# A two-layer model on one core: how queries and keys are split into three bf16 parts in the second layer

## What is computed

```python
def _L1_attn_ref(x, spectral_basis, W_qkv, W_out, a, b, dt):
    ...
    def fhn_dynamics(stimulus, a, b, dt, n_steps=N_FHN_STEPS, tau=TAU, threshold=THRESHOLD):
        ...
        for _ in range(n_steps):
            dv_explicit = v - v * v * v / 3.0 - w + I
            v_next = v + dt * dv_explicit
            w_next = (w + alpha * (v_next + a)) / denom
            v = jnp.clip(v_next, -3.0, 3.0)
            w = jnp.clip(w_next, -3.0, 3.0)
        response = v * stim_scale
        ...
            scores = jnp.einsum('bhtd,bhsd->bhts', q_c, k_c) * scale
            probs = jax.nn.softmax(scores, axis=-1)
            attn_energy = probs.sum(axis=-1)
            stim = jnp.broadcast_to(attn_energy[..., None], (B, H, e - s, Dh))
            fhn_out, fhn_state = fhn_dynamics(stim, a, b, dt)
            fhn_gate = jax.nn.sigmoid(fhn_out.mean(axis=-1))[..., None]
            probs = probs * (0.5 + 0.5 * fhn_gate)
            probs = probs / (probs.sum(axis=-1, keepdims=True) + 1e-08)
            out_chunks.append(jnp.einsum('bhts,bhsd->bhtd', probs, v_c))
...
x = L0_attn_x                       # 16 x 512 x 128, float32
xn = _layernorm(x, axis=-1)
x = x + _L0_attn_ref(xn, ...) + _L0_ffn_ref(xn, ...)
xn = _layernorm(x, axis=-1)
x = x + _L1_attn_ref(xn, ...) + _L1_ffn_ref(xn, ...)
return x
```

## Time and profile before

| | |
|---|---|
| median of 3 runs | 1517.55 us (1516.59 to 1521.41) |
| profiled execution | 1515.43 us |
| its span, first to last instruction | 1513.5 us |
| TensorE, VectorE, ScalarE, GpSimd busy | 93%, 78%, 54%, 35% |
| mean granted TensorE clock | 0.984 |

### The profile page before, as it was taken

The page is one execution under the profiler, slowest core; times in us unless marked ns, Lnnn a source line. Parts: engine busy times, 40 slices in busy tenths (PEclk is TensorE's granted clock), DMA queues, the critical chain, the costliest instruction groups (busy, mean ns, idle before and its releaser), DMA issues.

```text
span 1513.5 us, 35393 instructions
## 1 busy us (share of the span) xinstructions
PE 1404.1 (93%) x12926; PEld 904.6 (60%) x12926; DVE 1177.3 (78%) x2687; ACT 817.2 (54%) x1562; POOL 523.3 (35%) x942
## 2 busy tenths in 40 slices
PE   5699999999999899999998999999999999999994
PEld 3467677677776799998884444444444444444432
DVE  4789889889888795456677888888888888888752
ACT  2334534544543333334334677777766777776673
POOL 2333234234233111172312244444434444442121
PEclk8999999999999999999999999999999999999997
DMA  4111111111112566776973444333334443332300
GB/s 119 38 42 52 45 48 44 51 47 44 54 33 66 165 208 209 220 245 208 258 195 62 98 106 105 98 98 102 87 93 102 108 103 97 98 92 70 82 9 14
DMA packets 118205, 151.94 MB, mean 100 GB/s; under 512 B 31269, under 2 KB 83109, under 8 KB 113413
## 3 DMA queue, kind: packets, MB, share of 16 engines
q1 hardware_dynamic: 105160, 119.47, 29.0%
q0 software_dynamic: 12880, 30.30, 6.8%
HBM read 108.35 MB, written 40.83 MB: 99 GB/s over the span
## 4 chain that ended last, share of the span: by engine, by line
PE 48%; DVE 32%; POOL 7%; issue 6%; ACT 5%; DMA 1%; SPq 0%; POOLq 0%; DVEq 0%; ACTq 0%
DVE nmax L1516 8%; PE bank L1948 8%; PE bank L1939 8%; DVE P L1205 7%; PE bank L1816 5%; PE bank L1994 5%; PE bank L2017 4%; ACT P L946 3%; PE bank L1773 3%; PE bank L1850 2%; PE bank L1957 2%; PE bank L1864 2%; DVE t L1080 1%; PE bank L2064 1%; DVE t L1078 1%
## 5 line engine op out<-in xcount | busy, mean ns | idle before, releaser
L1516 DVE TENSOR_REDUCE nmax<-bank 128x1 f32<-128x512 f32 (+3 forms) x704 | 428.8, 634 | 84.6 <-PE bank L1994 83.6
L946 ACT ACTIVATE P<-bank 128x512 f32<-128x512 f32 x640 | 371.2, 599 | 183.2 <-PE bank L2017 178.4
L1994 PE MATMUL bank<-KT,QT 76*128 76x512 bf16 (+3 forms) x1024 | 251.3, 303 | 28.5 <-DVE nmax L1516 20.9
L2017 PE MATMUL bank<-QT,KT 78*128 78x512 bf16 (+3 forms) x1024 | 244.5, 301 | 8.9 <-ACT P L946 5.5
L693 POOL DMA_INDIRECT xs_d<-xn,idx x128 | 124.6, 973 | 306.0 <-PE bank L1773 197.9
L1994 PEld LDWEIGHTS bank<-KT,QT 76*128 76x128 bf16 x1024 | 86.8, 97 | 189.1 <-DVE nmax L1516 130.6
L1816 PE MATMUL bank<-P,V 128*32 128x512 f32 (+3 forms) x2048 | 191.3, 447 | 0.0
L1205 DVE TENSOR_TENSOR P<-bank,early_w 128x512 f32<-128x512 f32 x256 | 158.7, 682 | 41.3 <-PE bank L1773 41.2
L910 ACT ACTIVATE hr<-bank 128x512 f32<-128x512 f32 x142 | 84.8, 597 | 175.0 <-PE bank L1939 172.1
L741 POOL DMA_INDIRECT hT<-ys_d,idx x104 | 103.5, 995 | 159.9 <-PE bank L2017 141.8
L2017 PEld LDWEIGHTS bank<-QT,KT 78*128 78x128 bf16 x1024 | 98.6, 98 | 85.0 <-ACT P L946 31.9
(11 more groups left out here) (257 smaller groups left out, 2228.6 us busy)
## 6 DMA issues: line engine op xcount, KB each, us to landing
QT<-parts_d SPq DMA_DIRECT2D x96, 192.0 KB
P<-in_fc SPq DMA_DIRECT2D x71, 256.0 KB, 2.9
P<-in_proj SPq DMA_DIRECT2D x71, 256.0 KB, 3.2
parts_d<-parts SPq DMA_DIRECT2D x32, 384.0 KB, 2.5
P<-xs_d SPq DMA_DIRECT2D x71, 128.0 KB, 3.0
ys_d<-P POOLq DMA_DIRECT2D x71, 128.0 KB, 3.4
KT<-parts_d SPq DMA_DIRECT2D x64, 128.0 KB
KT<-parts_d SPq DMA_DIRECT2D x32, 192.0 KB
```

Source lines behind the costliest of these rows:

```text
L946: nc.scalar.activation(P[s % 2][:, u, :], bank[k % 2][:, :], ACT.Exp, scale=float(DH) ** -0.5).then_inc(s_sb, 1)
L1516: nc.vector.tensor_reduce(nmax[:, s // TWO, h:h + TWO * nh - 1:TWO, j], max_bank(n, k)[:, 0:nh * w].rearrange("p (h w) -> p h w", h=nh), A ...
L1994: ins = pe.matmul(max_bank(n, k)[:, i * w:(i + 1) * w], QT[n.p][0:MROWS, h, j * 128:(j + 1) * 128], KT[n.p][0:MROWS, h, 0:w], start=True, ...
L2017: ins = pe.matmul(bank[k % 2][:, c:c + n], KT[b.p][0:SROWS, h, 128 * kb:128 * kb + 128], QT[b.p][0:SROWS, h, 128 * kb:T], start=True, stop ...
```

## The change

In the loop, `take_part` and `lo2` are gone. ScalarE copies the bank to `t1` in float32 (`raw2`, at (1,7) and (1,9)). GpSimd subtracts the high part from `t1` in place (`residue_of`, both c, after the gather at unit 16 and ahead of `fhn_two_steps`). `mid2` casts `t1` in place of the bank, at its old places. VectorE subtracts the middle part (`low2`, an old function) after maxima 23 and 25. The bank is free for its next writers after `raw_part`. `raw2` of a batch waits for `lo_part` of the batch before, as `t1` has one copy for each c. `minus` and its constant are gone too. The expert stage's two batches keep their way.

```diff
@@ -170,7 +170,6 @@
         parts = [sb(f"parts{c}", [128, 3, T], BF16) for c in range(2)]
-        minus = sb("minus", [128, 128], BF16)
         yb = [sb("yb0", [128, J, H, DH + 1]), early_w[:, 2 * T:2 * T + J * H * (DH + 1)].rearrange("p (j h c) -> p j h c", j=J, h=H)]
@@ -255,8 +254,7 @@
         k_sheets, half_consts, rows_ordered, sheets_known = sem("k_sheets"), sem("half_consts"), sem("rows_ordered"), sem("sheets_known")
-        hi_part, res_part, mid_part, low_ps, lo_part = (sem(s) for s in ("hi_part", "res_part", "mid_part", "low_ps", "lo_part"))
-        minus_ready = sem("minus_ready")
+        hi_part, res_part, mid_part, raw_part, lo_part = (sem(s) for s in ("hi_part", "res_part", "mid_part", "raw_part", "lo_part"))
         parts_stored = [sem(f"parts_stored{c}") for c in range(2)]
@@ -343,7 +341,9 @@
 
-            return (res_part if n.less(L2 + 2) else lo_part), n.at(2, c + 1 - 2 * L2)
+            if n.less(L2 + 2):
+                return res_part, n.at(2, c + 1 - 2 * L2)
+            return raw_part, n.at(2, c + 1 - 2 * (L2 + 2))
 
@@ -777,6 +777,12 @@
 
+            def residue_of(n, c):
+
+                pool.wait_ge(hi_part, n.at(2, c + 1 - 2 * L2))
+                pool.wait_ge(raw_part, n.at(2, c + 1 - 2 * (L2 + 2)))
+                nc.gpsimd.tensor_tensor(t1[c][:, :], t1[c][:, :], parts[c][:, 0, :], ALU.subtract).then_inc(res_part, 1)
+
             def body2(b):
@@ -785,6 +791,9 @@
                 gather_at(b + 3, b, [(4, 16)])
+                if within(b + 2):
+                    for c in range(2):
+                        residue_of(b + 2, c)
                 if within(b + -1) and (b + -1).known() < LAST:
@@ -917,11 +926,12 @@
                 act.wait_ge(res_part, n.at(2, c + 1 - 2 * L2))
-                nc.scalar.copy(parts[c][:, 1, :], t1[c][:, :] if n.less(L2 + 2) else qk_bank(n, c)[:, :]).then_inc(mid_part, 1)
-
-            def lo2(n, c):
-                act.wait_ge(low_ps, n.at(2, c + 1 - 2 * (L2 + 2)))
-                nc.scalar.copy(parts[c][:, 2, :], qk_bank(n, c)[:, :]).then_inc(lo_part, 1)
+                nc.scalar.copy(parts[c][:, 1, :], t1[c][:, :]).then_inc(mid_part, 1)
+
+            def raw2(n, c):
+                if not n.less(L2 + 3):
+                    act.wait_ge(lo_part, n.at(2, c - 1 - 2 * L2))
+                nc.scalar.copy(t1[c][:, :], qk_bank(n, c)[:, :]).then_inc(raw_part, 1)
 
@@ -1023,8 +1033,8 @@
                             mid2(b + 2, u // 2)
-                        if at in ((2, 4), (2, 6)) and front:
-                            lo2(b + 2, u // 2 - 2)
+                        if at in ((1, 7), (1, 9)) and front:
+                            raw2(b + 2, u // 2 - 3)
                         if at == (2, 8) and after:
@@ -1389,7 +1399,6 @@
                     second_layer_consts()
-                    nc.vector.tensor_scalar(minus[:, :], ident[:, :], -1.0, None, ALU.mult).then_inc(minus_ready, 1)
 
@@ -1650,6 +1659,8 @@
                         ln(b + 2, False, range(2 * (m - 11), 2 * (m - 11) + 2))
+                    if m in (23, 25) and front:
+                        low2(b + 2, (m - 23) // 2)
                     if m == 34 and after:
@@ -1956,13 +1967,6 @@
 
-            def take_part(n, c, k):
-
-                pe.wait_ge(minus_ready, 1)
-                pe.wait_ge((hi_part, mid_part)[k], n.at(2, c + 1 - 2 * L2))
-                pe.matmul(qk_bank(n, c)[:, :], minus[:, :], parts[c][:, k, :], start=False, stop=True,
-                          skip_group_check=True).then_inc((res_part, low_ps)[k], 1)
-
             def v_rows(n):
@@ -2143,10 +2147,6 @@
                             q_rows(b + 2, u - 4)
-                        if where in ((1, 8), (2, 0)) and front:
-                            take_part(b + 2, s - 1, 0)
-                        if where in ((2, 2), (2, 4)) and front:
-                            take_part(b + 2, u // 2 - 1, 1)
                         if where == (2, 6) and after:
```

## The result

The changed kernel takes 1553.15 us (median of 4 runs, 1540.9 to 1558.68) against 1517.07 for the kernel before: a ratio of 1.0232, 95% interval 1.0204 to 1.026, so 36 us slower. The forecast was 1542. The forecast's own range was 1534 to 1554, so the median lies just inside its upper end. The runs of the changed kernel scatter by 18 us, those of before by 7. The profiled execution took 1558.3 us, with a span of 1556.6 against 1513.5; it is the second slowest of the four.

What follows compares the result with a forecast made beforehand. The prediction took ScalarE's queue followed by GpSimd's FHN steps as the bound; 0.87 + 0.43 + 0.55 = 1.85 us in 13 bodies made 24 us, giving 1539.5, or about 1542 in terms of the median, range 1534 to 1554.

Steps and rivals of the forecast that it cites:

- What bounds: Between unit (1,6) and VectorE's reciprocal in a steady body, ScalarE's queue followed by GpSimd's FHN steps sets the time.
- Spare time of 1.3 us: TensorE's and VectorE's path beside the FHN chain has 1.3 us to spare a body, read from VectorE idling before L1560.
- late exponentials: TensorE's score products wait for exponentials delayed by the copies: about 0.5 us on its path, inside the 1.3 to spare.
- Removed products, at nothing: Four take_part products a body, units (1,8) to (2,4), 0.88 us of TensorE, lie beside the chain and gain nothing.
- Body b = L2, at nothing: The loop's first body, without FHN steps, changes by between -0.9 and +1.0 us, taken as 0.
- Copies ahead of the gate, 0.83: Two raw2 copies at (1,7) and (1,9) in ScalarE's queue make tanh_gate start 0.83 us later.
- Residues, 1.22 us each, and 0.87 for copies and residues together: GpSimd's two subtractions ahead of fhn_two_steps take 1.22 us each; with the copies they move L390 0.87 us later.
- Contention, 0.43 and 0.55: GpSimd stands still while VectorE's low2 reads two SBUF inputs: the first low2 adds 0.43 us, the second 0.55.
- VectorE's own time, at nothing: Two low2 after maxima 23 and 25, 1.2 us of VectorE a body, fit in spare time and cost nothing.
- The sum: 0.87 + 0.43 + 0.55 = 1.85 us a body on the chain, in 13 bodies, 24 us.
- the late start without contention: Rival, chance 0.2: VectorE and GpSimd read side by side, leaving 13 x 0.87 = 11 us, time 1529.
- dear residues: Rival, chance 0.1: residues take 1.8 us each or mid casts wait for GpSimd, 0.65 more a body, time 1551.

Runs made afterwards that it cites:

- early gate: The kernel before with only tanh_gate moved from (2,1) to (1,8) on ScalarE: 1509.6 us against 1516.0, ratio 0.9958.
- filler kernel: The changed kernel with eight unread 256-column TensorE products a body put back at the places of the removed four: 1549.38 us against 1516.63, ratio 1.0229.
- the copies alone: The kernel before plus two unread float32 copies of 128x512 on ScalarE at (1,7) and (1,9): 1528.28 us against 1516.0, ratio 1.0082.
- the kernel with two reads: The kernel before plus two unused VectorE subtractions a body, both inputs in SBUF, after maxima 23 and 25: 1526.57 us, run once.
- two reductions: The kernel before plus two unused VectorE reductions a body, one SBUF input each, after maxima 23 and 25: 1521.01 us, run once.

## Why the prediction was right in its sign and its chain, and where it was off

**What bounds.** Right. The FHN steps behind ScalarE's queue set the end of the body: moving the gate shortens it, taking the products away doesn't.

**Spare time of 1.3 us.** Wrong, and it is the step that failed most clearly. I read VectorE's idle time in front of L1560 as the slack of everything beside the FHN steps. The early gate shows 0.27. It did little harm here, as the new chain moved by 1.39 and stayed the longer one. The late exponentials, put at 0.5 us on the path beside it, cost more as well: two copies make the first body, which has no gate, 0.78 us longer.

**Removed products, at nothing.** Right (0.06 us a body).

**Body b = L2, at nothing.** Wrong by a little: at full clock it takes 43.05 in place of 42.32 (filler kernel), 0.7 us more.

**Copies ahead of the gate, 0.83.** Right: the gate moved by 0.86, and the copies alone cost 0.95.

**Residues, 1.22 us each, and 0.87 for copies and residues together.** Right in size: 1.16 measured (L784), and 0.91 for the two together when contention is taken out.

**Contention, 0.43 and 0.55.** The mechanism is right, the size was not: 0.48 in all, not 0.98. In the changed kernel L390 moved by 1.20, so the first `low2` cost about 0.3: it stretched L388 by 0.45, but L390 would have waited for the gate for part of that, and starts 0.86 us after L388 in place of the 0.55 of the kernel where `low2` reads the bank. The residue that was under way when this `low2` began wasn't stretched (1.16 us in both kernels); `low2` itself took 0.82 in place of 0.68. The second cost 0.18, since GpSimd's L395 was under way when it came, ran to its end, and only the rest of `low2` lay over L397. In the kernel with two reads the VectorE instruction came first by 0.04 us and GpSimd paid the full 0.52. The Trainium skill, SBUF — State Buffer, section Who interferes with whom, says that whoever issues first keeps the shared ports. These cases agree with it; the one in the earlier trace rows that doesn't is a GpSimd step of 4 elements that had started 0.11 us ahead.

**VectorE's own time, at nothing.** Right: 43.59 with two reductions.

**The sum.** Forecast 1.85 a body in 13 bodies, 24 us; measured 1.39 in 13 bodies and 0.7 in body b = L2, 19 us. The other 17 us of the median are put down to the granted clock, of which the prediction said nothing for the loop: it took the 1.00 of the earlier trace rows over. That term, put at nothing, is the largest error in the time. That the total came near is luck, two misses of opposite sign: 6 us too many for contention and 17 too few for the clock. Of the rivals, the late start without contention (1529) gave too little, and dear residues (1551) the right time for a wrong reason.

## What to carry to other kernels

Idle time of one engine in front of one instruction bounds the slack of that instruction only; move the instruction before and see how far the body really follows. Ask of an added instruction what is queued behind it, more than how long it takes: two copies ahead of the gate cost 0.95 us a body, and 0.88 us of TensorE's products beside the chain 0.06. And look at a new wait of TensorE twice, once for its length and once for the clock that may fall after it.

## What the runs showed that I had not expected

Waits of TensorE of 0.5 and 0.3 us close together, or one of 0.8, in a loop that had run at clock 1.00, were followed in some bodies by 3 to 17 us at 1.2 GHz, and by 20 in one body of the changed kernel with the early gate. In 13 bodies of the changed kernel's profiled execution falls made 25 us, one of the eight, about 4 us, without such a wait. A kernel with a body nearly as long (44.53, the two copies) kept its clock; one of 44.10, with two reads of SBUF on VectorE and a wait of 0.64 us, lost it in two bodies of twelve. The order in time speaks for the waits as the cause; no experiment removed them alone. What decides in which body the clock falls stays open.

A GpSimd subtraction of 128x512 took 1.02 us with two float32 inputs (2.05 for two) and 1.16 with one of them in bf16.
